# A causal mask added by TensorE: identity tiles of 64x128 or of 64x64

## The chip, the core and the metric

The kernel runs on one core of one Trainium2 chip. The metric is the device time of one execution in microseconds (us), lower being better. TensorE multiplies: a weight load (PEld in the profile) puts the stationary operand into the array, a matmul (PE) streams the moving operand's columns past it and writes PSUM. VectorE (DVE), ScalarE (ACT) and GpSimd (POOL) do the rest.

## The reference

Two decoder layers on x of shape (4, 512, 128). The first has causal self-attention with 16 heads of 8 features, cross-attention to 154 context rows, and a gated mixture of 8 experts. The second has chunked linear attention, cross-attention with 8 heads of 128, and a gated feed-forward part of 384. After each of the six parts stands a residual sum and a layer norm. What matters here is the first part:

```python
scores = jnp.einsum('bshd,bthd->bhst', q / jnp.sqrt(Hd).astype(q.dtype), k)
future = jnp.triu(jnp.ones((S, S), dtype=bool), 1)
scores = jnp.where(future[None, None, :, :], jnp.finfo(scores.dtype).min, scores)
attn = jax.nn.softmax(scores, axis=-1)
ctx = jnp.einsum('bhst,bthd->bshd', attn, v)
```

## The kernel before, in words

All matrix work goes through one TensorE instruction stream, whose order is written out by hand: a string of letters (`MERGE`) merges sixteen streams of steps, and a second string (`BANK_OF`) gives each step its PSUM bank. The steps of one batch's self-attention, another batch's cross-attention and the later layers of earlier batches are interleaved. Each engine walks the same list of steps and waits on two semaphores per PSUM bank, one that says filled and one that says drained.

Self-attention is computed twice for each batch b and each group g of four heads. `scores` (step "S", lines 1120 and 1126) computes queries by keys, from which VectorE takes row maxima (line 1818). `scores_T` (step "ST", lines 1147 and 1153) computes keys by queries, which ScalarE turns into exponentials (line 1557) and `values` (line 1179) multiplies by V. The self-attention groups are 16 (4 batches, 4 groups). Each has five steps of either kind, and these hold eight pieces: two pairs of heads times four blocks of 128 rows (`SELF_PIECES`, `SELF_T_PIECES`; three of the five steps hold two pieces each). Cross-attention's steps call the same two functions with a=1, on lines 1120, 1147 and 1138, and add no mask.

A piece is made of products in bf16 that contract over 64 partitions, so that r=0 uses partitions 0 to 63 and r=1 partitions 64 to 127, and the two write different PSUM banks (`to[:, r]`). First come the two score products, one for each r, 128 to 512 columns wide, with 128 weight columns (shape 64x128). Four mask products follow, which add -1e30 above the diagonal of the 128x128 diagonal block by accumulation in PSUM: for each half e of the block and each r, the weights are `ident2[p, e, :]`, a 64x128 tile that has an identity in its half e and zeros in the other, and the moving operand is a part of `maskS` or `maskT`, 128 columns for one e and 64 for the other. Every mask product thus writes all 128 PSUM partitions, adding zeros in one half. Each product has its own weight load.

TensorE is used in four shapes in this kernel: 128x128 (f32 products and transposes), 64x128 (scores and masks), 128x32 (lines 1166, 1179, 1265 and 1294) and 64x32 (line 1138, the last 26 context rows of cross-attention's transposed scores, which can come right before or behind steps of the other kinds). Line 1064 is the transposing helper, 1188 a transpose of maxima in bf16, 1207 an output product.

Of the kernel before, what the change touches and what calls it, by code (L numbers as in the profile page):

```python
# [17 lines left out]
P = 128  # L18
# [20 lines left out]
TILE = P // 2  # L39
R = range(2)  # L40
# [368 lines left out]
def build(nc, x, ctx_1024, L0_attn_W_qkv, L0_attn_q_scale, L0_attn_k_scale, L0_attn_W_out,  # L409
# [8 lines left out]
    with ExitStack() as stack:  # L418
        def sb(name, shape, dt=F32):
            return stack.enter_context(nc.sbuf_tensor(name, shape, dt))  # L420
# [11 lines left out]
        def pair(key):  # L432
            k = place[key][0]
            return psum[:, k:k + 2, :]
# [36 lines left out]
        def placed_until(b):  # L471
            return 16 * (2 * SLOTS * (b + 1) + max(0, b - 1))
# [20 lines left out]
        ident2 = sb("ident2", [P, 2, P], BF16)  # L493
        maskS = sb("maskS", [P, 2, P], BF16)
        maskT = sb("maskT", [P, 2, P], BF16)
# [111 lines left out]
        for z, of in enumerate(halves):  # L607
# [3 lines left out]
            at = HS * h  # L611
# [427 lines left out]
        def _(pe):  # L1039
            def fill(key):  # L1040

                for k, n in sorted(earlier[key]):
                    pe.wait_ge(bank_drained[k], n + 1)
                return bank(key)

            def fills_(ins, key):
                return ins.then_inc(bank_filled[place[key][0]], 1)

            mm = nc.tensor.matmul
# [58 lines left out]
            def scores(b, a, g, u):  # L1108
                if a == b == u == g == 0:
                    pe.wait_ge(consts_ready, 1)  # L1110
                if u == g == 0:
                    pe.wait_ge(cross_placed if a else qk_placed, placed_until(b))
                key = (b, "S", a, g, u)
                fill(key)
                to = pair(key)
                for at, jj, q in PIECES[a][u]:
                    n = C if a else P * (q + 1)
                    for r in R:
                        p = slice(TILE * r, TILE * r + TILE)
                        last = mm(to[:, r, at:at + n], Q6[a][p, b % 2, 2 * g + jj, P * q:P * q + P],  # L1120
                                  K6[a][p, b % 2, 2 * g + jj, 0:n], start=True, stop=bool(a))
                    for e in (() if a else (1, 0)):

                        for r in R:
                            p = slice(TILE * r, TILE * r + TILE)
                            last = mm(to[:, r, at + n - P + TILE * e:at + n], ident2[p, e, :],  # L1126
                                      maskS[p, e, TILE * e:P], start=False, stop=e == 0)
                fills_(last, key)

            def scores_T(b, a, g, u):  # L1130
                if u == 0:
                    pe.wait_ge(max_placed[a], 16 * (NQ * b + g + 1))
                key = (b, "ST", a, g, u)
                to = fill(key)
                if a and u == 2:
                    for h in range(4):
                        p = slice(TILE * (h % 2), TILE * (h % 2) + TILE)
                        last = mm(to[32 * h:32 * h + 32, :], K6[1][p, b % 2, 2 * g + h // 2, P:CP],
                                  Q6[1][p, b % 2, 2 * g + h // 2, :], start=True, stop=True)
                    fills_(last, key)  # L1140
                    return
                to = pair(key)
                for at, jj, k in ([(0, u, 0)] if a else SELF_T_PIECES[u]):
                    n = S - P * k
                    for r in R:
                        p = slice(TILE * r, TILE * r + TILE)
                        last = mm(to[:, r, at:at + n], K6[a][p, b % 2, 2 * g + jj, P * k:P * k + P],  # L1147
                                  Q6[a][p, b % 2, 2 * g + jj, P * k:S], start=True, stop=bool(a))
                    for e in (() if a else R):

                        for r in R:
                            p = slice(TILE * r, TILE * r + TILE)
                            last = mm(to[:, r, at:at + TILE * (e + 1)], ident2[p, e, :],  # L1153
                                      maskT[p, e, 0:TILE * (e + 1)], start=False, stop=e == 1)
                fills_(last, key)

            def values(b, a, g):
# [269 lines left out]
            def down(b, h):  # L1427
# [4 lines left out]
                for i in range(2):  # L1432
# [3 lines left out]
                fills_(last, key)  # L1436

            work = {"qkv": qkv, "qkT": qkT, "S": scores, "ST": scores_T, "PV": values,
                    "mT": max_T, "cT": products_T, "ctxT": ctx_T, "out": out_product,
                    "wT": setup_T, "wM": setup_products, "xk": cross_k, "xv": cross_v,  # L1440
# [715 lines left out]
```

## Time and profile before

| | |
|---|---|
| Median of the timed runs (3) | 490.84 us (489.36 to 491.09) |
| Span of the profiled execution | 1523.4 us |
| Its own time | no other than its span is known |
| TensorE products, busy in the profile | 1509.8 us in 4432 instructions |
| VectorE, ScalarE, GpSimd busy | 405.0, 370.9 and 184.6 us |
| Mean granted TensorE clock in the profile | 1.000 |

The profile comes from one execution. It spans 3.1 times as long as the timed runs took, though the clock it records is the full one. Times of VectorE and ScalarE in it fit into 490.84 us; those of TensorE do not. So its times of TensorE can't be set beside the runs as they stand. In the order of time, a row merges neighbouring instructions of one line; its first number is the start, its second the time to the modelled end of the last one. Ends of matmuls are modelled, so the distance between starts is the better measure.

### The profile page before, as it was taken

Reading aid. Unit: us, or ns where it says so; the run is one execution under the profiler, and the core shown is the slowest. Engines: PE = TensorE matmul, PEld = TensorE weight load, DVE = VectorE, ACT = ScalarE, POOL = GpSimd, SP = SyncE. Lnnn points to the kernel's source line nnn. Section 1 sums busy time; section 2 is a strip of 40 time slices with the busy share of each in tenths; the row PEclk is TensorE's granted clock in tenths of the full one; section 3 lists DMA queues with packets and bytes.
Section 4 is the critical chain, followed back from the end, with each engine's and each line's share of the span. In section 5 each row is a group of like instructions: output and inputs, shape, how many; then the busy total and the mean of one; then the engine's idle time right before and its main releaser. Section 6 shows DMA issues by size and latency. Waiting matters only on the chain.

```text
span 1523.4 us, 12413 instructions
## 1 busy us (share of the span) xinstructions
PE 1509.8 (99%) x4432; PEld 813.3 (53%) x4432; DVE 405.0 (27%) x1147; ACT 370.9 (24%) x879; POOL 184.6 (12%) x349
## 2 busy tenths in 40 slices
PE   7999999999999999999999999999999999999998
PEld 4545654433453454557553444556543745784786
DVE  2433223333222333212223222122221231111112
ACT  2223222221322232221122223222212232313111
POOL 4200012000301101101001001111011122011111
DMA  5110000100000000000010000100000000000000
GB/s 145 31 43 1 9 6 22 34 18 7 1 21 12 11 12 11 1 1 5 1 32 1 1 0 3 27 1 1 4 4 0 1 0 0 0 1 1 0 0 14
DMA packets 27185, 18.40 MB, mean 12 GB/s; under 512 B 8217, under 2 KB 26773, under 8 KB 26997
## 3 DMA queue, kind: packets, MB, share of 16 engines
q1 hardware_dynamic: 23413, 15.44, 3.8%
q10 hardware_dynamic: 3712, 2.17, 0.6%
q8 instruction: 36, 0.59, 0.2%
q14 instruction: 24, 0.20, 0.0%
HBM read 5.58 MB, written 1.05 MB: 4 GB/s over the span
## 4 chain that ended last, share of the span: by engine, by line
PE 99%; DVE 0%; ACT 0%; POOL 0%; issue 0%; POOLq 0%; ACTq 0%; DVEq 0%
PE psum L1064 14%; PE psum L1179 9%; PE psum L1389 8%; PE psum L1325 7%; PE psum L1412 7%; PE psum L1120 6%; PE psum L1147 6%; PE psum L1423 5%; PE psum L1169 4%; PE psum L1166 3%; PE psum L1099 3%; PE psum L1434 3%; PE psum L1126 3%; PE psum L1153 3%; PE psum L1281 2%; PE psum L1207 2%
## 5 line engine op out<-in xcount | busy, mean ns | idle before, releaser
L1557 ACT ACTIVATE EX<-psum 128x1024 f32<-128x1024 f32 (+1 forms) x128 | 122.6, 971 | 155.4 <-PE psum L1153 109.9
L1179 PE MATMUL psum<-EX,V 128*32 128x256 f32 (+3 forms) x512 | 133.4, 1284 | 0.0
L1120 PE MATMUL psum<-K,Q 64*128 64x154 bf16 (+4 forms) x512 | 129.9, 595 | 0.5 <-DVE nmax L1813 0.5
L1147 PE MATMUL psum<-Q,K 64*128 64x512 bf16 (+3 forms) x320 | 126.2, 803 | 0.0
L1818 DVE TENSOR_REDUCE nmax<-psum 128x2 f32<-128x768 f32 (+1 forms) x96 | 79.9, 866 | 130.8 <-PE psum L1126 130.4
L1813 DVE TENSOR_REDUCE nmax<-psum 128x4 f32<-128x616 f32 (+1 forms) x80 | 68.5, 882 | 126.9 <-PE psum L1120 100.2
L1389 PE MATMUL psum<-GP,xT 128*128 128x308 f32 x96 | 102.0, 1264 | 0.0
L1412 PEld LDWEIGHTS psum<-VM,REST 128*128 128x128 f32 x192 | 80.4, 555 | 5.2 <-issue 3.2
L1412 PE MATMUL psum<-VM,REST 128*128 128x128 f32 x192 | 82.5, 662 | 0.0
L1325 PE MATMUL psum<-ew,xT 128*128 128x512 f32 x48 | 81.0, 1932 | 0.0
L1179 PEld LDWEIGHTS psum<-EX,V 128*32 128x32 f32 x512 | 36.5, 217 | 79.7 <-issue 75.7
L1120 PEld LDWEIGHTS psum<-K,Q 64*128 64x128 bf16 x512 | 35.2, 142 | 80.9 <-issue 78.6
L1153 PEld LDWEIGHTS psum<-maskT,ident 64*128 64x128 bf16 x512 | 55.4, 208 | 35.8 <-issue 34.1
L2045 DVE TENSOR_REDUCE nxmax<-psum 128x2 f32<-128x308 f32 x64 | 30.6, 479 | 164.8 <-PE psum L1389 164.8
L1153 PE MATMUL psum<-maskT,ident 64*128 64x64 bf16 (+1 forms) x512 | 74.4, 407 | 0.0
L1461 ACT COPY pvraw<-psum 128x512 f32<-128x512 f32 x32 | 18.7, 585 | 228.0 <-PE psum L1179 135.1
L1126 PE MATMUL psum<-maskS,ident 64*128 64x64 bf16 (+1 forms) x512 | 73.5, 407 | 0.0
L1126 PEld LDWEIGHTS psum<-maskS,ident 64*128 64x128 bf16 x512 | 53.5, 203 | 37.6 <-issue 35.7
L1022 POOL TENSOR_TENSOR GP<-REST,xrs 128x512 f32<-128x512 f32 (+1 forms) x48 | 32.5, 700 | 262.7 <-PE psum L1064 224.0
L1423 PE MATMUL psum<-xT,fT 128*128 128x256 f32 x72 | 62.1, 1101 | 0.0
L1640 ACT ACTIVATE REST<-psum,nxmax 128x154 f32<-128x154 f32 x96 | 36.5, 385 | 102.3 <-DVE nxmax L2045 99.5
L1389 PEld LDWEIGHTS psum<-GP,xT 128*128 128x128 f32 x96 | 42.2, 465 | 31.7 <-issue 30.4
(345 smaller groups left out, 2042.0 us busy)
## 6 DMA issues: line engine op xcount, KB each, us to landing
Q<-xparts SPq DMA_DIRECT2D x24, 128.0 KB
Q<-parts SPq DMA_DIRECT2D x21, 128.0 KB
K<-parts SPq DMA_DIRECT2D x21, 128.0 KB
X<-in_x SPq DMA_DIRECT2D x4, 256.0 KB, 3.0
Q<-in_L_xattn_Wkv SPq DMA_DIRECT2D x1, 1024.0 KB, 7.3
K<-xkparts SPq DMA_DIRECT2D x24, 38.5 KB
out<-XB_rest SPq DMA_DIRECT2D x6, 128.0 KB, 1.8
Q<-in_L_xattn_Wq SPq DMA_DIRECT2D x1, 512.0 KB, 4.4
```

The lines of the kernel that those rows point to most:

```text
L1064: last = nc.tensor.transpose(to[0:n, at:at + m], src, ident[0:m, 0:m])
L1120: last = mm(to[:, r, at:at + n], Q6[a][p, b % 2, 2 * g + jj, P * q:P * q + P], K6[a][p, b % 2, 2 * g + jj, 0:n], start=True, stop=bool(a))
L1126: last = mm(to[:, r, at + n - P + TILE * e:at + n], ident2[p, e, :], maskS[p, e, TILE * e:P], start=False, stop=e == 0)
L1147: last = mm(to[:, r, at:at + n], K6[a][p, b % 2, 2 * g + jj, P * k:P * k + P], Q6[a][p, b % 2, 2 * g + jj, P * k:S], start=True, stop=bool(a))
L1153: last = mm(to[:, r, at:at + TILE * (e + 1)], ident2[p, e, :], maskT[p, e, 0:TILE * (e + 1)], start=False, stop=e == 1)
L1179: last = mm(to[32 * h:32 * h + 32, P * k:S], V[:, k, 4 * g + h, :], EX[:, ex_slot(b, a, g, u) + h % 2, at:at + n], start=k == PV_ORDER[0], ...
L1325: fills_(mm(fill(key), half_of(b, h).xT[2][:, P * i:P * i + P], ew[:, 4 * side:4 * side + 4, :].rearrange("p e d -> p (e d)")), key)
L1389: fills_(mm(fill(key)[:, 0:2 * C], half_of(b, h).xT[4][:, P * q:P * q + P], G[:, head:head + 2, :].rearrange("p h c -> p (h c)")), key)
L1412: mm(to, of.XPT[:, head, :], VM[:, head, :], start=head == 0, stop=False)
L1423: last = mm(to[:, HS * w:HS * w + HS], fT[:, w, P * c:P * c + P], half_of(b, h).xT[5])
L1557: drains(nc.scalar.activation(dst, src, ACT.Exp), key)
L1818: last = vec.tensor_reduce(nmax[:, :, jj, q], src[:, :, at:at + P * (q + 1)], AX.X, ALU.max, negate=True)
```

## The change

The mask products of both kinds of scores use the 64x64 identity `ident2[p, 0, 0:TILE]` as weights. The product of half e writes only the 64 PSUM partitions of that half (`half`), with the same moving columns as before. Its number of products and loads stays, and so do all waits and the order of steps. In `scores` the order of the halves turns from (1, 0) to (0, 1), and each product now ends its own accumulation.

```diff
@@ scores @@
-                    for e in (() if a else (1, 0)):
+                    for e in (() if a else R):
 
                         for r in R:
-                            p = slice(TILE * r, TILE * r + TILE)
-                            last = mm(to[:, r, at + n - P + TILE * e:at + n], ident2[p, e, :],
-                                      maskS[p, e, TILE * e:P], start=False, stop=e == 0)
+                            p, half = [slice(TILE * i, TILE * i + TILE) for i in (r, e)]
+                            last = mm(to[half, r, at + n - P + TILE * e:at + n], ident2[p, 0, 0:TILE],
+                                      maskS[p, e, TILE * e:P], start=False, stop=True)
...
@@ scores_T @@
                         for r in R:
-                            p = slice(TILE * r, TILE * r + TILE)
-                            last = mm(to[:, r, at:at + TILE * (e + 1)], ident2[p, e, :],
-                                      maskT[p, e, 0:TILE * (e + 1)], start=False, stop=e == 1)
+                            p, half = [slice(TILE * i, TILE * i + TILE) for i in (r, e)]
+                            last = mm(to[half, r, at:at + TILE * (e + 1)], ident2[p, 0, 0:TILE],
+                                      maskT[p, e, 0:TILE * (e + 1)], start=False, stop=True)
```

## Rows read from the trace of the kernel before

**Rows 1.** The page: the span, busy time of each engine, and the chain that ended last.

```profile
span 1523.4 us, 12413 instructions
...
PE 1509.8 (99%) x4432; PEld 813.3 (53%) x4432; DVE 405.0 (27%) x1147; ACT 370.9 (24%) x879; POOL 184.6 (12%) x349
...
PE 99%; DVE 0%; ACT 0%; POOL 0%; issue 0%; POOLq 0%; ACTq 0%; DVEq 0%
```

**Rows 2.** Busy time and (x) instructions of each engine in two stretches.

```profile
50.00:805.00 755.00, 754.54 (x2825) 381.09 (x2825) 226.28 (x565) 191.47 (x366) 68.70 (x123) 1.00 0.05 13
805.00:1523.40 718.40, 713.04 (x1505) 410.49 (x1503) 159.89 (x523) 168.27 (x491) 90.09 (x181) 1.00 0.01 3
```

**Rows 3.** TensorE in order of time, 701.1 to 702.7 us: start, duration, operation.

```profile
701.15 0.70 PE L1147 MATMUL psum<-Q,K 64*128 64x384 bf16 x2
701.53 0.71 PE L1153 MATMUL psum<-maskT,ident 64*128 64x64 bf16 x4
701.92 0.53 PE L1147 MATMUL psum<-Q,K 64*128 64x128 bf16 x2
702.13 0.55 PE L1153 MATMUL psum<-maskT,ident 64*128 64x64 bf16 x4
702.62 0.52 PE L1207 MATMUL psum<-xwo,ctxT 128*128 128x128 f32 x1
...
701.16 0.10 PEld L1153 LDWEIGHTS psum<-maskT,ident 64*128 64x128 bf16 x2
...
702.62 0.22 PEld L1207 LDWEIGHTS psum<-xwo,ctxT 128*128 128x128 f32 x1 [0.23 <-issue]
```

**Rows 4.** Groups by shape: the mask products, their weight loads, the 64x32 loads' line.

```profile
L1423 PE MATMUL psum<-xT,fT 128*128 128x256 f32 x72 | 62.1, 1101 | 0.0
...
L1153 PE MATMUL psum<-maskT,ident 64*128 64x128 bf16 x256 | 57.6, 433 | 0.0
L1126 PE MATMUL psum<-maskS,ident 64*128 64x128 bf16 x256 | 57.0, 433 | 0.0
...
L1126 PE MATMUL psum<-maskS,ident 64*128 64x64 bf16 x256 | 50.2, 381 | 0.0
...
L1126 PEld LDWEIGHTS psum<-maskS,ident 64*128 64x128 bf16 x512 | 53.5, 203 | 37.6 <-issue 35.7
```

**Rows 5.** TensorE in order of time, 61.2 to 62.3 us, products and loads.

```profile
62.03 0.56 PE L1126 MATMUL psum<-maskS,ident 64*128 64x64 bf16 x4
62.27 0.95 PE L1120 MATMUL psum<-K,Q 64*128 64x384 bf16 x2
...
62.04 0.10 PEld L1126 LDWEIGHTS psum<-maskS,ident 64*128 64x128 bf16 x2 [0.74 <-issue]
62.07 0.25 PEld L1120 LDWEIGHTS psum<-K,Q 64*128 64x128 bf16 x2
```

**Rows 6.** TensorE in order of time around a switch of shape, at 627.07 us.

```profile
626.59 0.55 PE L1126 MATMUL psum<-maskS,ident 64*128 64x64 bf16 x4
627.07 0.91 PE L1138 MATMUL psum<-Q,K 64*32 64x512 bf16 x4
...
627.07 0.10 PEld L1138 LDWEIGHTS psum<-Q,K 64*32 64x32 bf16 x4 [0.23 <-issue]
```

**Rows 7.** TensorE in order of time around two more switches, at 340.46 and 561.42 us.

```profile
339.62 0.91 PE L1138 MATMUL psum<-Q,K 64*32 64x512 bf16 x4
340.46 0.70 PE L1120 MATMUL psum<-K,Q 64*128 64x384 bf16 x2
...
559.74 1.75 PE L1147 MATMUL psum<-Q,K 64*128 64x512 bf16 x4
561.42 0.91 PE L1138 MATMUL psum<-Q,K 64*32 64x512 bf16 x4
```

**Rows 8.** Waits: who waited for whom, us in total, times, longest.

```profile
DVE nmax L1818 <- PE psum L1126: 130.4, 46, 10.1
ACT EX L1557 <- PE psum L1153: 109.9, 76, 12.4
```

## The prediction

> **What bounds the kernel now.** I read the page first [rows 1]. TensorE is busy for 1509.8 us of a span of 1523.4 us, and the chain that ended last is TensorE for 99%. It looks like a plain TensorE bound. But the timed runs took 490.84 us, so this chain can't be theirs. VectorE (405.0 us) and ScalarE (370.9 us) would fit into such a run; TensorE would not. Something in the profiled execution slowed TensorE alone.
>
> How much, the order of time tells [rows 3]. The pair of L1147 with 128 columns starts at 701.92 and the next one at 702.13: 0.21 us for 128 columns that both row halves stream at once. At the granted clock that is recorded, 1.00 [rows 2], its level of 2.4 GHz, 128 columns are 128/2400 = 0.053 us. So the profiled execution feeds TensorE at about a quarter, 0.21/0.053 = 3.9 times slower. The f32 products keep the same ratio if an f32 column counts as two: L1423 has 256 columns and takes 62.1/72 = 0.86 us, four times 0.21 [rows 4]. I estimate TensorE's streaming in an unslowed run as 1509.8/3.9 = 387 us. That is 79% of 490.84, with 104 us left for the start, waits and gaps between products. VectorE is busy for 405 us of the same run, nearly as much.
>
> By stretch [rows 2]: the mask products run from about 42 to 875 us of the profile. In 50 to 805 us, TensorE has 754.5/3.9 = 193 us of streaming by this estimate, VectorE 226 and ScalarE 191 us. No engine is far ahead there. All three are fed by the same TensorE queue, since VectorE's maxima and ScalarE's exponentials wait for the last mask product of a step [rows 8]. Behind 805 us nothing is changed (but for the last 70 us of L1153).
>
> I sum against the profiled execution's own time, its span of 1523.4 us, and separately against the runs' median, 490.84 us, because the two differ by 3.1 times and a gap of TensorE counts differently in them.
>
> **The change, part by part.**
>
> *Count.* 16 groups of 8 pieces in two kinds of scores make 256 diagonal blocks, each with four mask products and four loads. The 512 and 512 products stay, and so do their moving columns, 64 for one half and 128 for the other. VectorE, ScalarE, the DMA queues, waits and buffers are untouched. Swapping the halves' order and ending each accumulation cost nothing: the same four instructions stand in a row and nobody reads between them.
>
> *What it can save.* Before, the two row halves stream side by side, but the halves e come one behind the other, because both use all 128 weight columns. After it, the four products use four different quarters of the array. If those run at once, the 64 columns lie beside the 128. That frees 64/2400 = 0.027 us for each block, 256 x 0.027 = 6.8 us in an unslowed run. [Rows 5] bear the size out: the loads of the second pair of mask products start at 62.04, the loads behind that pair at 62.07, 0.03 us later. In the profiled execution the saving is 64 columns at 0.21/128, or 0.105 us a block and 27 us in all. Below, it is nothing, if the quarters don't overlap. I take the full saving, since four products of 64x32 start together in the trace and cost no more than 512 columns, 0.84 us from 339.62 to 340.46 [rows 7].
>
> *What it adds.* Every block now leaves the shape 64x128 for 64x64, and mostly returns. It enters 256 times. It goes back to a 64x128 product 200 times; the other blocks are followed by another shape anyway. (96 returns lie inside steps of two pieces, three in each of 32 lists; the other 104 I counted in the order of the trace.) That makes 456 new switches; there were 265 before. How do switches look? Inside a shape, loads run ahead: L1153's loads start at 701.16, just behind the pair of L1147 that started at 701.15 and streams until 701.53 [rows 3]. At a switch they don't. The load for L1207 starts at 702.62 together with its product, and so does that of L1138 at 627.07 [rows 3, 6]. Its load line has stood idle 0.23 us. The four mask products ahead of those two switches take 0.48 and 0.49 us, where the same four products inside the shape take 0.39 (701.53 to 701.92) or 0.24 us (62.03 to 62.27) [rows 3, 5, 6]. So a switch holds the next product back by about 0.48 - 0.39 = 0.09 us until the earlier one has run out. The nearest of these is L1126 to L1138, from 64x128 to 64x32, the same rows with fewer weight columns, just what this change does.
>
> *Bounds.* From below, nothing. Two pairs of 512 columns and the switch behind them take 561.42 - 559.74 = 1.68 us, exactly two times 0.84, and the exit from 64x32 costs nothing either [rows 7]. What the switch held back there was given back behind it: with TensorE fed at a quarter, the gap falls into time in which it would have stood still. An unslowed TensorE has no such time, so I don't carry this zero over, though I can't exclude it. From above, the 104 us that streaming leaves over, if all of it went into the 265 present switches: 0.39 us each. I take 0.09 us, the row that is nearest in kind. Then the new switches cost 456 x 0.09 = 41 us of TensorE, less 6.8 us saved: 34 us more.
>
> The Trainium skill, "TensorEngine Tiling (Array Packing)", section Key Properties, says that changing the tiling mode, and not just the tile, drains the TensorE. By that rule each of the 456 switches costs a drain; the trace agrees as far as the held-back loads go. The page gives no duration.
>
> *From TensorE's time to the run's.* In the attention part TensorE goes from an estimated 193 us of streaming, and present gaps, to 34 us more; VectorE has 226 us there. Where TensorE is what others wait for, all of the 34 us count. Where VectorE is behind, a part is absorbed by its backlog, but TensorE also waits for it through the PSUM banks. With busy times so even I take a little over half, 0.55: 34 x 0.55 = 19 us. 490.84 + 19 = **510 us**, 3.9% slower. With everything counted it is 525 us; with switches at 0.05 us and half of that counted, 490.84 + (23 - 7)/2 = 499 us. The nothing above for other engines rests on their queues being unchanged: if TensorE's gaps are hidden by VectorE, what is late next is VectorE's maxima at L1818.
>
> For the profiled execution, if it is slowed again in the same way, the sum is different. The gaps vanish in the slow feed and only columns count: 1523.4 - 27 = about 1496 us. So the profile may get shorter while the runs get longer.
>
> **The rivals.**
>
> *The overlap wins (faster).* Switches cost nothing at full speed either, as in [rows 7], or under 7/456 = 0.015 us each, the point where this case turns. For it: the zero sums just named, and four products of 64x32 running at once. Against it: the loads that stand idle at a switch. All saved streaming would give 490.84 - 7 = 484 us. If the mask pairs now cost more than their columns, as the 0.39 us for 192 columns in [rows 3] hints, a saving of a tenth of a microsecond in profile time on every block more, at 490.84/1523.4, adds 8 us: 476 us. I give this 0.20.
>
> The same page of the Trainium skill, section Overview, lists 64x64 as four independent tiles; by that alone the time would be the 484 us of this rival.
>
> *Hidden (no change).* TensorE's gaps are covered in the timed runs, because VectorE and ScalarE set the pace of the attention part; 226 against 193 us in [rows 2] speaks for it, the many short waits of both for mask products [rows 8] against it. The time would be 489 to 493 us. 0.09.
>
> *Only a part is done.* If the quarters don't overlap, there is no saving, only switches: 41 x 0.55 = 23 us, 514 us. It is inside the forecast's own range and gets its chance from it.
>
> *The drain is longer.* At 0.2 us for a switch, 91 us of TensorE with most of it counted: 560 us. Half of the 104 us would have to be switches now. 0.06.
>
> **How the numbers follow.** The forecast has 0.65 and its own range is 497 to 526 us. With the faster rival (0.20), no change (0.09) and the long drain (0.06), the range that leaves out at most 2 in 10 goes from 482 to 528 us: it leaves out the long drain and the lower part of the faster rival. A measurement of this kernel can tell about 0.5% from no change. Faster by more than that gets 0.20; within it 0.10, with 0.01 for the lower edge of the forecast; slower 0.70.
>
> **What would show it.** Right: in the order of time, loads of both the 64x64 mask products and the 64x128 products behind them start together with their product and not ahead of it. The four mask products of a block start within some 0.02 us. The group rows show 512 products each with loads of 64x64, and a profiled span near 1496 us if slowed again. If the profile is not slowed, the page should show TensorE with short idle times at each change of shape. Wrong: loads of 64x64 that run ahead during the score products, which would take the switch's price away; or pairs of mask products that still start one behind the other, which would take the saving away. A time under 488 us would say that the price of a switch, and not the conversion, was the failed step.

## The result, and the profile after

The changed kernel takes 530.08 us (526.5 to 532.28, 4 runs), the kernel before 490.66 us (489.36 to 491.09, 4 runs). The ratio is 1.0786, with an interval of 1.0748 to 1.0824: 39 us slower. The direction was forecast, the size was not. 510 us were predicted, with a range of 482 to 528.

This profile was taken with TensorE at its full feed, that is with its columns streaming at the granted clock and not at a quarter of it: it spans 527.4 us, close to its runs. The slowed profile of the kernel before can't be set beside it, so I ran the kernel before once more for a profile at full feed. Its base rows, with those of the changed kernel, answer to [rows 1]. The page of the changed kernel (the last row is the granted clock in 40 slices, in tenths):

```profile
span 527.4 us, 12413 instructions
...
PE 504.2 (96%) x4432; PEld 318.1 (60%) x4432; DVE 390.8 (74%) x1147; ACT 348.5 (66%) x879; POOL 188.1 (36%) x349
...
PEclk9669999999999969999999999999999999999998
```

The page of the kernel before, run again:

```profile
span 490.2 us, 12413 instructions
...
PE 460.3 (94%) x4432; PEld 309.3 (63%) x4432; DVE 387.6 (79%) x1147; ACT 345.2 (70%) x879; POOL 188.2 (38%) x349
...
PEclk9599999989999999999999999999999999999999
```

TensorE is busy for 504.2 us instead of 460.3, 43.9 us more with the same 4432 instructions. The span grows by 37.2 us. VectorE (390.8 against 387.6 us) and ScalarE (348.5 against 345.2 us) hardly do more. Even before, TensorE was busy for 94% of the span.

Where it went, the stretches tell, which answer to [rows 2]. Columns are the stretch, its length, then busy time and instructions of TensorE's products, its loads, VectorE, ScalarE and GpSimd, then the granted clock. The changed kernel:

```profile
0.00:30.00 30.00, 17.25 (x82) 11.56 (x82) 13.79 (x54) 10.41 (x20) 21.76 (x41) 0.82 0.81 213
30.00:317.00 287.00, 284.89 (x2900) 162.47 (x2900) 227.51 (x585) 186.72 (x382) 76.85 (x132) 0.97 0.13 34
317.00:527.40 210.40, 202.06 (x1458) 144.10 (x1456) 149.53 (x509) 151.42 (x478) 89.47 (x177) 0.99 0.04 11
```

The kernel before, run again, cut at about the same points of the work, some 15 us ahead of the last mask product. That one starts at 295.3 us here and at 332.5 us in the changed kernel, 37.2 us later, which is all that the span grew by:

```profile
0.00:30.00 30.00, 18.53 (x98) 12.72 (x98) 14.79 (x55) 10.60 (x20) 21.66 (x41) 0.83 0.77 205
30.00:280.00 250.00, 240.00 (x2848) 151.65 (x2850) 221.34 (x578) 181.86 (x379) 76.68 (x132) 0.99 0.15 40
...
280.00:490.20 210.20, 201.79 (x1490) 144.88 (x1484) 151.49 (x516) 152.75 (x481) 89.86 (x178) 1.00 0.04 11
```

Behind the cut, both take 210 us. All of the loss is in the attention part, 287 us in place of 250. That part held TensorE busy for 240 of 250 us before the change, and for 284.9 of 287 after it.

How a block looks, in TensorE's order of time, which answers to [rows 3, 5, 6]. The changed kernel first; the three last rows are weight loads:

```profile
61.21 0.34 PE L1120 MATMUL psum<-K,Q 64*128 64x384 bf16 x2
61.48 0.24 PE L1126 MATMUL psum<-maskS,ident 64*64 64x128 bf16 x4
61.65 0.23 PE L1120 MATMUL psum<-K,Q 64*128 64x128 bf16 x2
61.81 0.24 PE L1126 MATMUL psum<-maskS,ident 64*64 64x128 bf16 x4
61.99 0.39 PE L1147 MATMUL psum<-Q,K 64*128 64x512 bf16 x2
...
61.47 0.11 PEld L1126 LDWEIGHTS psum<-maskS,ident 64*64 64x64 bf16 x4 [0.17 <-issue]
61.65 0.10 PEld L1120 LDWEIGHTS psum<-K,Q 64*128 64x128 bf16 x2
61.81 0.11 PEld L1126 LDWEIGHTS psum<-maskS,ident 64*64 64x64 bf16 x4
```

The kernel before, run again, with its loads in the two last rows:

```profile
50.77 0.39 PE L1120 MATMUL psum<-K,Q 64*128 64x512 bf16 x2
51.00 0.25 PE L1126 MATMUL psum<-maskS,ident 64*128 64x64 bf16 x4
51.08 0.38 PE L1120 MATMUL psum<-K,Q 64*128 64x512 bf16 x2
51.30 0.25 PE L1126 MATMUL psum<-maskS,ident 64*128 64x64 bf16 x4
...
50.78 0.31 PEld L1126 LDWEIGHTS psum<-maskS,ident 64*128 64x128 bf16 x4
51.03 0.10 PEld L1120 LDWEIGHTS psum<-K,Q 64*128 64x128 bf16 x2
```

Take the pair of 128 columns that starts at 61.65. Its mask products start at 61.81, 0.16 us later. 128 columns are 0.053 us at the clock's level of 2.4 GHz, so 0.11 us are added: the mask's loads start at 61.81 too and no longer run ahead. Over all 256 blocks, the mask's first load starts 1 to 2 ns ahead of its product in the changed kernel, and 54 to 216 ns ahead in the kernel before. The 384 columns from 61.21 take 0.27 us, again 0.11 more than their 0.16. Before, the mask's loads start at 50.78, just behind the score pair of 50.77, and the mask products follow 0.23 us later, behind 512 columns (0.213 us).

The way back costs as much. The four mask products start within 0.01 us of each other at 61.48, and the next score pair starts at 61.65, 0.17 us later, for 128 columns that would take 0.053 us. Before, the four took 0.08 us (51.00 to 51.08), 64 and 128 columns one behind the other. Per block with both switches that is 0.11 + 0.09 = 0.20 us more; the 0.027 us that the overlap saves is in it already. The medians over the whole trace say the same more exactly. A pair of 128 columns takes 0.056 us to the next start before and 0.160 us after, 0.104 more. The four mask products with a 64x128 product behind them take 0.085 us before, and 0.176 us (maskS) or 0.183 us (maskT) after, about 0.095 more. With 256 ways in and 199 ways back found in the trace, that is 256 x 0.104 + 199 x 0.095 = 45.5 us, and the attention part's busy time grew by 44.9. The Trainium skill, "TensorEngine Tiling (Array Packing)", section Key Properties, has the rule that a change of the tiling mode drains the TensorE; these rows agree with it (to drain: to let what is under way run out before the next product starts): products and loads behind a switch start about 0.1 us later than the columns alone would have it. They show it for a change from 64x128 to 64x64, with the same 64 rows.

The kernel before has such switches too. This one, from 64x128 to 64x32, is of the kind of [rows 7] at 561.42, now at full feed:

```profile
121.83 0.39 PE L1147 MATMUL psum<-Q,K 64*128 64x512 bf16 x2
122.15 0.40 PE L1138 MATMUL psum<-Q,K 64*32 64x512 bf16 x4
```

It takes 0.32 us for 512 columns, again 0.10 us more than the 0.216 us that such a pair takes inside its shape.

Who waits for the mask products now, from the list of waits (total, times, longest), which answers to [rows 8]. The changed kernel:

```profile
ACT EX L1557 <- PE psum L1153: 22.4, 29, 2.7
...
DVE nmax L1818 <- PE psum L1126: 13.9, 17, 3.9
...
DVE nmax L1813 <- PE psum L1126: 5.5, 8, 1.7
```

The kernel before, run again:

```profile
ACT EX L1557 <- PE psum L1153: 7.4, 12, 2.6
...
DVE nmax L1818 <- PE psum L1126: 3.6, 8, 0.7
```

VectorE's and ScalarE's waits for masks grow from 11.5 us (0.5 of them at L1813) to 41.8 us.

### The profile page after: what moved, and what is told of

It reads as the page before. It is cut to its first block and busy times, and to the rows that moved or that the text cites. A ratio compares the mean times of both kernels' runs of the same rounds, so it can differ in the third digit from the quotient of the medians.

```text
span 527.4 us, 12413 instructions
## 1 busy us (share of the span) xinstructions
PE 504.2 (96%) x4432; PEld 318.1 (60%) x4432; DVE 390.8 (74%) x1147; ACT 348.5 (66%) x879; POOL 188.1 (36%) x349
## 5 line engine op out<-in xcount | busy, mean ns | idle before, releaser
L1813 DVE TENSOR_REDUCE nmax<-psum 128x4 f32<-128x616 f32 (+1 forms) x80 | 67.9, 877 | 9.1 <-PE psum L1126 5.5
L1120 PE MATMUL psum<-K,Q 64*128 64x154 bf16 (+4 forms) x512 | 56.3, 271 | 4.2 <-DMA K<-parts 3.1
L1147 PE MATMUL psum<-Q,K 64*128 64x512 bf16 (+3 forms) x320 | 51.8, 326 | 0.8 <-DVE nmax L1818 0.5
L1120 PEld LDWEIGHTS psum<-K,Q 64*128 64x128 bf16 x512 | 20.2, 94 | 30.8 <-issue 20.3
L1179 PE MATMUL psum<-EX,V 128*32 128x256 f32 (+3 forms) x512 | 37.7, 435 | 0.0
L2045 DVE TENSOR_REDUCE nxmax<-psum 128x2 f32<-128x308 f32 x64 | 28.7, 469 | 5.7 <-PE psum L1389 5.4
L1153 PE MATMUL psum<-maskT,ident 64*64 64x64 bf16 (+1 forms) x512 | 32.4, 229 | 0.0
L1126 PE MATMUL psum<-maskS,ident 64*64 64x128 bf16 (+1 forms) x512 | 31.6, 229 | 0.0
L1389 PE MATMUL psum<-GP,xT 128*128 128x308 f32 x96 | 30.5, 432 | 0.0
L1153 PEld LDWEIGHTS psum<-maskT,ident 64*64 64x64 bf16 x512 | 14.6, 104 | 19.6 <-issue 13.7
L1147 PEld LDWEIGHTS psum<-Q,K 64*128 64x128 bf16 x320 | 15.1, 93 | 17.2 <-issue 6.5
L1179 PEld LDWEIGHTS psum<-EX,V 128*32 128x32 f32 x512 | 14.5, 109 | 18.0 <-issue 17.2
L1325 PE MATMUL psum<-ew,xT 128*128 128x512 f32 x48 | 25.2, 662 | 0.0
L1412 PE MATMUL psum<-VM,REST 128*128 128x128 f32 x192 | 23.8, 277 | 0.2 <-DVE VX L1917 0.2
```

The source lines that it names most:

```text
L1126: last = mm(to[half, r, at + n - P + TILE * e:at + n], ident2[p, 0, 0:TILE], maskS[p, e, TILE * e:P], start=False, stop=True)
L1153: last = mm(to[half, r, at:at + TILE * (e + 1)], ident2[p, 0, 0:TILE], maskT[p, e, 0:TILE * (e + 1)], start=False, stop=True)
L1179: last = mm(to[32 * h:32 * h + 32, P * k:S], V[:, k, 4 * g + h, :], EX[:, ex_slot(b, a, g, u) + h % 2, at:at + n], start=k == PV_ORDER[0], ...
L1389: fills_(mm(fill(key)[:, 0:2 * C], half_of(b, h).xT[4][:, P * q:P * q + P], G[:, head:head + 2, :].rearrange("p h c -> p (h c)")), key)
L1412: mm(to, of.XPT[:, head, :], VM[:, head, :], start=head == 0, stop=False)
L1813: last = vec.tensor_reduce(nmax[:, :, :, q], src[:, :, 0:2 * n].rearrange("p r (j k) -> p r j k", j=2), AX.X, ALU.max, negate=True)
```

## The experiments

Theory 1: each switch of TensorE's shape costs about 0.106 us (the expectations use this figure; the medians above give 0.104 on the way in), and since TensorE is the engine that the attention part waits for, most of it reaches the run. Theory 2: 64x64 products are slow in themselves, by their loads or their issue. A second question is how much of a microsecond of TensorE reaches the run, since the prediction's 0.55 was clearly too small. All ratios are against the kernel before, run on the same chip between them.

**The kernel before again (again).** No edit.

> The kernel before, unchanged, for a profile in which TensorE is not slowed. Theory 1 (switches of shape cost TensorE about 0.106 us each, as the changed kernel's profile has it) expects the four mask products of a block to take 0.08 to 0.09 us between starts when 64x128 products follow, a score pair of 128 columns 0.05 to 0.06 us, and no gap at either. Theory 2 (64x64 products are slow in themselves, by their loads or their issue) expects the same here; the rows are the base for both. Time 490.7 us, span about 488 us.

Measured: 491.73 us, ratio 1.0006 (0.9987 to 1.0025), span 490.2 us. The rows above are its rows, and they are as expected: 0.08 us for four mask products.

**One kind of score alone (s_only, t_only).** The change's two hunks, one at a time.

s_only has the hunk in `scores` as in the change and `scores_T` as before; t_only has it the other way round.

> Only the products that add maskS (the scores for VectorE's maxima) use 64x64 tiles; those that add maskT stay 64x128. Theory 1: about half of the 456 switches, 128 entries and 99 returns, so half of the 39 us: 510 us, and the same share of TensorE's added time reaches the run in either half. Rival: the loss sits in one of the two chains alone, by a late maximum or a late exponential; then this is either about 491 or about 530 us.

> Only the products that add maskT (the transposed scores for ScalarE) use 64x64 tiles. With maskS alone the time rose by 16.3 us, the whole change by 39.1. If TensorE's waits absorb a few us of added time once, whichever part adds it, this run rises by 16 to 18 us as well, to about 508 us, and the two halves together give more than their sum. If the transposed scores are the dearer ones in themselves, it rises by the rest, 23 us, to 514 us.

Measured: 507.24 us, ratio 1.0331 (1.0292 to 1.0369), for maskS alone, and 507.90 us, ratio 1.0338 (1.0312 to 1.0365), for maskT alone. So neither chain alone bears the loss: 16.3 and 17.1 us against the kernel before of their calls. The sum, 33 us, is 6 us under the whole change's 39. I took this for a few us that are absorbed once. The runs of mask2 below speak against that reading. By the medians above, the halves add 22 and 23 us to TensorE, so a share of 0.73 and 0.74 reaches their times.

**Everything in 64x64 (all64).** The score products of self- and cross-attention are cut into quarters as well.

```diff
-                    for r in R:
-                        p = slice(TILE * r, TILE * r + TILE)
-                        last = mm(to[:, r, at:at + n], Q6[a][p, b % 2, 2 * g + jj, P * q:P * q + P],
+                    for e, r in [(e, r) for e in R for r in R]:
+                        p, half = [slice(TILE * i, TILE * i + TILE) for i in (r, e)]
+                        last = mm(to[half, r, at:at + n],
+                                  Q6[a][p, b % 2, 2 * g + jj, P * q + TILE * e:P * q + TILE * e + TILE],
                                   K6[a][p, b % 2, 2 * g + jj, 0:n], start=True, stop=bool(a))
...
```

> The score products too are cut into 64x64 quarters (four in place of two, self and cross), so that no block changes shape inside; the mask products are those of the changed kernel. Theory 1 (the switch is what costs): the 456 added switches are gone and the four quarters run side by side, so 485 to 495 us. Theory 2 (64x64 products and their loads are slow in themselves): there are even more of them, so 530 us or above.

Measured: 491.56 us, ratio 1.0017 (0.9990 to 1.0045). The same mask products that cost 39 us cost nothing that can be measured once the products around them have their shape, with 832 more products in all (5264 in place of 4432). Its order of time, two pieces of 512 columns, and the loads below:

```profile
51.87 0.41 PE L1120 MATMUL psum<-K,Q 64*64 64x512 bf16 x4
52.10 0.22 PE L1127 MATMUL psum<-maskS,ident 64*64 64x128 bf16 x4
52.14 0.40 PE L1120 MATMUL psum<-K,Q 64*64 64x512 bf16 x4
52.36 0.24 PE L1127 MATMUL psum<-maskS,ident 64*64 64x64 bf16 x4
...
52.11 0.12 PEld L1120 LDWEIGHTS psum<-K,Q 64*64 64x64 bf16 x4
52.14 0.13 PEld L1127 LDWEIGHTS psum<-maskS,ident 64*64 64x64 bf16 x4
```

The loads of the score products of 52.14 start at 52.11, during the mask products, and the masks take 0.04 us to the next start. Nothing is drained here. Theory 2 falls, and with it the idea that the 64x64 loads matter. In this trace the shape changes 330 times, as often as in the kernel before; in the changed kernel it changes 785 times.

**The same products, regrouped (grouped, grouped_old).** In steps of two pieces, both pieces' scores come first and then both pieces' masks. For this the second piece's score products continue the bank's accumulation in place of starting one.

```diff
                 for at, jj, q in PIECES[a][u]:
...
-                                  K6[a][p, b % 2, 2 * g + jj, 0:n], start=True, stop=bool(a))
+                                  K6[a][p, b % 2, 2 * g + jj, 0:n], start=bool(a) or at == 0,
+                                  stop=True, skip_group_check=not a)
+                for at, jj, q in PIECES[a][u]:
+                    n = C if a else P * (q + 1)
                     for e in (() if a else R):
...
```

> The changed kernel, but in the steps of two pieces both pieces' score products come first and then both pieces' mask products. The same products, loads and columns; 96 entries and 96 returns of the 456 added switches go. Theory 1 (0.106 us of TensorE for a switch, 0.85 of it in the run): 192 x 0.106 x 0.85 = 17 us less than the changed kernel's 530.1, so 513 us. Theory 2 (64x64 products are slow in themselves): 530 us.

> The control of the regrouping: the same order of products with 64x128 mask products, so no switch is saved. Both theories: 491 us, within 1%. Should it be clearly faster, the regrouping has a gain of its own that has to be taken off the regrouped 64x64 kernel.

Measured: 503.99 us, ratio 1.0275 (1.0237 to 1.0313), for the 64x64 masks, and 490.86 us, ratio 0.9996 (0.9979 to 1.0012), for the control. Leaving out 192 of the 456 added switches takes 26 us back, and the regrouping gives nothing of its own. The control leaves out no switch and gains nothing. By switches alone 17 us were expected, so the direction is as forecast and the size is not. TensorE is busy for 476.9 us there, 27.3 less than in the changed kernel; the switches left out account for some 22 us by the medians (0.104 in, 0.12 out). A part of the rest is probably the clock (below): its median over the runs is 0.982 against 0.968, some 4 us by the line given there. Another 5 us or so of the 26 stay open.

**More mask products in the same shape (mask3, mask2, after3).** The mask is added three times, twice, and, in the changed kernel, three times.

```diff
-                    for e in (() if a else (1, 0)):
+                    for i, e in enumerate(() if a else (1, 0) * 3):
...
-                                      maskS[p, e, TILE * e:P], start=False, stop=e == 0)
+                                      maskS[p, e, TILE * e:P], start=False, stop=i == 5)
...
```

> The kernel before with each block's mask products issued three times (the mask is added three times), all in the shape 64x128. It adds 2 x 0.084 us x 256 = 43 us of TensorE streaming without a single switch. If nearly all TensorE time in this part reaches the run (0.86 of it, as 39 of 46 us did in the changed kernel): 528 us. If 0.55 of it does, as I had predicted, and the switches cost more than their rows show: 514 us.

> The kernel before with each block's mask products issued twice, all 64x128: half of the added TensorE time of the kernel that issues them three times, 256 x 0.085 = 22 us there by the rows, 20.5 us by columns. If a fixed few us of added time are absorbed and the rest counts in full, less than half of the 31.8 us come back: 11 to 14 us, 502 to 505 us. If a constant share of 0.78 counts, 16 us: 507 us.

> The changed kernel with each block's four 64x64 mask products issued three times (the mask is added three times). No switch is added; two more fours of products a block in the same shape. If the four run side by side, each costs 0.055 us: 2 x 256 x 0.055 = 28 us of TensorE and, nearly all of it counting now, 553 to 558 us. If 64x64 products were slow in themselves (0.17 us for each four, as between a block's starts in the changed kernel): 87 us, above 600 us.

Measured: mask3 522.77 us, ratio 1.0628 (1.0599 to 1.0658), 31.8 us for 41 us of columns (512 added fours, each with a pair of 64 and a pair of 128 columns at 2.4 GHz, 0.080 us), a share of 0.78. In the trace, each further four takes 0.085 us to the next start and not 0.080; by that it is 43.5 us and a share of 0.73. mask2 506.83 us, ratio 1.0306 (1.0278 to 1.0335), 15.3 us for 20.5, a share of 0.75 (0.70 by the trace's 21.8 us). Half of the products give half of the time. The interval of mask2 is 13.7 to 16.5 us, where 11 to 14 were expected if a few us were absorbed once, so this looks like a constant share, and the explanation that I had for the two halves has little left.

after3: 553.04 us, ratio 1.1233 (1.1158 to 1.1307), 23 us above the changed kernel, at the lower edge of what was expected. Its order of time:

```profile
61.08 0.39 PE L1120 MATMUL psum<-K,Q 64*128 64x512 bf16 x2
61.40 0.35 PE L1126 MATMUL psum<-maskS,ident 64*64 64x128 bf16 x12
61.69 0.39 PE L1120 MATMUL psum<-K,Q 64*128 64x512 bf16 x2
62.01 0.35 PE L1126 MATMUL psum<-maskS,ident 64*64 64x128 bf16 x12
```

Twelve mask products take 0.28 to 0.29 us (61.40 to 61.69), where four take 0.17: each further four cost 0.055 us. That is 128 columns. The 64 columns of the other half do lie beside them, and within the shape 64x64 masks are cheaper than the 0.085 us of the old ones. So the saving is real, and it is the two switches around it that eat it up. The 512 further fours are 28.7 us of TensorE, of which 23 reached the run, 0.80.

**No mask at all (nomask).** The kernel before without its mask products. It computes attention that isn't causal, with everything else as it was.

```diff
...
-                    for e in (() if a else (1, 0)):
-
-                        for r in R:
-                            p = slice(TILE * r, TILE * r + TILE)
-                            last = mm(to[:, r, at + n - P + TILE * e:at + n], ident2[p, e, :],
-                                      maskS[p, e, TILE * e:P], start=False, stop=e == 0)
...
```

> The kernel before without any mask product, so attention is not causal in what it computes; everything else stays. It takes 0.085 us x 256 = 22 us off TensorE, and no switch is added or removed. Adding 41 us of the same products raised the time by 32 us, a share of 0.78. If the same share holds downward: 17 us less, 474 us. If TensorE's added time counts and its saved time doesn't, because VectorE (221 of the 250 us of this stretch) takes over: 480 to 489 us; that would also say why the kernel with quarters throughout and its shortened version gave nothing.

Measured: 486.11 us, ratio 0.9905 (0.9879 to 0.9931). The page and the attention part:

```profile
span 484.4 us, 10365 instructions
...
PE 442.9 (91%) x3408; PEld 280.2 (58%) x3408; DVE 385.4 (80%) x1147; ACT 343.0 (71%) x879; POOL 187.3 (39%) x349
...
30.00:276.00 246.00, 227.63 (x1925) 127.14 (x1926) 221.29 (x582) 181.78 (x382) 76.83 (x132) 0.98 0.15 39
```

Some 22 us of TensorE (256 times 0.085) are gone, and the run gains 4.9 us. The attention part takes 246 us in place of 250, with TensorE busy for 227.6 and VectorE for 221.3. So TensorE's time counts for 0.70 to 0.78 upward and for about 0.2 downward (4.9 of 22 us): the kernel before stands near the bend. The clock was a little lower here, 0.977 against 0.983; if the changed kernel's line (below) holds for this kernel, that hides some 2 us more, and the share is 0.3. What takes over below it isn't shown; VectorE, with 90% of the stretch, is the nearest, and with it the order in which the engines feed each other.

**Shorter quarters (cut64).** All64, and the quarter that is masked as a whole gets its -1e30 with no score product under it, by one more pair of 64-column products per block. The diff is against the changed kernel.

```diff
+                    for what in ("full", 1, 0, "edge1", "edge0"):
                         for r in R:
+                            e = {"full": 0, "edge1": 1, "edge0": 0}.get(what, what)
                             p, half = [slice(TILE * i, TILE * i + TILE) for i in (r, e)]
...
+                            if what in (0, 1):
+                                m = n - TILE * (1 - e)
...
```

> All self-attention scores and masks in 64x64, cross scores too, and the 64x64 quarter that is masked as a whole gets its -1e30 without the score product under it, so that each quarter of the array streams n + 64 columns in place of n + 128 for a block. Theory 1: no switch inside a block, and 64 columns fewer, 256 x 0.027 = 7 us of TensorE, 0.8 of it in the run, less the issue of two more products a block: 484 to 489 us, the first version below the kernel before. If a quarter can't start its next product before the others are through, nothing is saved: 491 to 497 us.

Measured: 492.21 us, ratio 1.0023 (1.0006 to 1.0040). TensorE is busy for 454.2 us, 6.1 less than before, but the time doesn't fall. With nomask, that is no surprise: TensorE's time saved here hardly counts. So the time doesn't tell whether a quarter can start its next product before the others are through. The traces do: two blocks of 512 columns with their masks, up to the start of the 128x32 product behind them, take 0.706 us in the kernel before, 0.661 us in all64 and 0.620 us in cut64 (medians of three such places in each). The shorter quarters save time of TensorE, which they couldn't if each had to wait for the others. No version beat the kernel before while computing all of it.

**The changed kernel again, for its clock (after_again).** No edit.

> The changed kernel, unchanged, for more of its runs with their granted clocks. In its first four runs the time rose from 526.5 to 532.3 us as the mean clock fell from 0.976 to 0.960; the kernel before has 0.98 to 0.985. If TensorE's half clock in the gappier stretches is a part of the loss, the median stays near 530 us and runs with a clock above 0.975 lie near 526 us, some 6 us less of the loss. If the clock is beside the point, time and clock are unrelated here.

Measured: 529.77 us, ratio 1.0772 (1.0732 to 1.0813). In the ten runs of the changed kernel, those with a mean granted clock of 0.976 or more took 526.5, 526.7 and 527.4 us; those below took 529.1 to 532.3. A line through the ten falls by 3.0 us for each 0.01 of clock. The kernel before has a median of 0.983 in the ten runs of again; carried on to there, the changed kernel would take 525 us. Where the clock is low, the profile of the changed kernel shows:

```profile
30.00:54.00 24.00, 23.36 (x244) 13.47 (x244) 18.66 (x34) 11.08 (x18) 6.20 (x8) 0.80 0.11 29
54.00:184.00 130.00, 128.67 (x1477) 68.77 (x1479) 104.38 (x261) 85.86 (x136) 29.79 (x45) 1.00 0.15 38
184.00:204.00 20.00, 20.00 (x175) 9.50 (x167) 12.81 (x35) 9.45 (x20) 4.54 (x7) 0.74 0.15 42
204.00:317.00 113.00, 112.86 (x1018) 70.73 (x1010) 91.67 (x258) 80.33 (x209) 36.32 (x73) 1.00 0.11 29
```

In 184 to 204 us the clock is 0.74, partly at its lower level of 1.2 GHz, though TensorE counts as busy for all of the 20 us; in 30 to 54 us it is 0.80. The kernel before has 0.99 over its whole attention part. So some 4 to 5 of the 39 us may come by way of the clock, as an estimate from that line; a run that holds the clock fixed was not made. The clock accounts for little of the 6 us by which the whole change exceeds the sum of its halves. Their clocks have medians of 0.982 (s_only) and 0.974 (t_only) against 0.968, which by the line is 0.3 and 2.7 against 4.5 us, so 1.5 of the 6. The rest is open.

## Why the prediction was wrong, point by point

- **What bounds the kernel.** "No engine is far ahead there" was the first error. I divided TensorE's 754.5 us by 3.9 and got 193 us, less than VectorE's 226. At full feed TensorE is busy for 240 of the 250 us. TensorE was busy for 460 us in all and not for 387, so 73 of the 104 us "left over" were not slack. The division turns columns into time, and it loses what a slow feed hides: the drains of the 265 switches that were there already, at about 0.11 us each, are some 29 of the 73 us. The factor was a little too large as well: a pair of 128 columns takes 0.056 us at full feed, so 0.21/0.056 = 3.75, and 1509.8/3.75 is 403 us. The rest of the 73 is not taken apart.
- **The conversion.** The step that followed from it failed: "I take a little over half, 0.55". By mask3, mask2 and the two halves, 0.70 to 0.78 of TensorE's added time reaches the run. The share of 0.85 (37.2 us of span for 43.9 us of busy time) is of another kind, since busy time on the page isn't added columns: mask3 has 30.8 us of span for 36.0 us of busy time, 0.86 too. The conversion alone doesn't explain the miss: the prediction's own upper case, "with everything counted", was 525 us.
- **The price of a switch.** TensorE's added time, 34 us, was the second term that was too small: the medians give 45.5 us and the page shows 43.9. The 0.09 us was 0.48 less 0.39, four mask products with and without a switch behind them. The slowed profile gives two values for the latter: in 114 of its 200 ways back to a score product it is 0.24 us, in 85 it is 0.39 or 0.40, and the prediction had a row of each. With 0.24 the price would have been 0.24 us, and nothing in the prediction decides between them. That 0.09 came near the truth was luck. At full feed it is 0.104 us on the way in and 0.12 us on the way out (0.176 or 0.183 less the 0.055 that four products take within the shape).
- **The zero from below** was rightly not carried over: at full feed the same change of L1147 to L1138 costs 0.10 us. Where it went in the slow feed isn't shown beyond the rows.
- **The count and the saving.** 456 switches hold (the trace of the changed kernel has 455 more than that of the kernel before), and so does the overlap, which is 0.03 us a block within the shape. The 0.03 us between two loads in [rows 5] did not bear its size out, since loads that run ahead don't time the columns, and in that profile 64 columns were put at 0.105 us; after3 does. all64 and grouped show that the switches bear the loss.
- **The clock** was put at nothing, without a reason. By the line above it is 4 to 5 us.
- **The sum redone.** 45.5 us of TensorE at 0.73, the share that mask3 gives with TensorE's time read in the same way, are 33 us, and with 4 to 5 us by the clock the time is 528 to 529 us, against 530 measured. With the predicted 34 us and the measured share it would have been 516 us, so the price and the clock are needed too.
- **The signs.** Loads that start together with their product, and four mask products within 0.02 us, came as forecast. Short idle times of TensorE at each change of shape did not: the page counts the drain as busy, 96% of the span.
- **The rivals.** "The overlap wins" was wrong at full feed; its reasons were the zero sums of a profile that was slowed. "Hidden" rested on 226 against 193 us and fell with it. "The drain is longer" had the right side, but its 0.2 us for a switch is nearly twice what the rows show.
- **The profile forecast for a slowed execution**, 1496 us, was not put to the test; no such execution came again.

## What to carry to other kernels

Smaller tiles lost 39 us here where their neighbours in TensorE's queue kept another shape, and neither lost nor gained where the whole stretch had the same (all64). So count the changes of shape that an edit adds, 0.10 to 0.12 us each in this kernel, before counting the columns that it saves, and ask whether TensorE's time saved would reach the run at all. Grouping products of one shape took 26 of the 39 us back. And where a profile's span is far from the runs, don't take an engine's slack from a division: run the same kernel again for a profile that fits, since what a slowed engine hides can be just what decides.

## What the runs showed of the hardware that I had not expected

- One execution of the kernel before fed TensorE at a quarter, 0.21 us for 128 columns against 0.053, with a recorded clock of 1.00, so that it spanned 1523.4 us; the same kernel took 490 us otherwise. Where a switch and what is ahead of it could be read together there (561.42 - 559.74 us), it cost nothing net. The cause isn't known.
- The granted clock can fall to 0.74 of full in a stretch in which TensorE counts as busy all the time (184 to 204 us of the changed kernel). Busy in the page includes the time in which it drains, so a TensorE at 96% isn't a TensorE that streams.
- The price isn't symmetric: the same 256 fours of mask products, 22 us of TensorE, cost 15.3 us when they were added (mask2) and gave 4.9 us when they were left out (nomask).
- In 64x64 the quarters of the array run on their own: streaming 64 columns fewer in each of them took 0.04 us off two blocks (cut64 against all64).
